# Attention and experts on one core: the chunk's steps in new orders on TensorE, VectorE, ScalarE and GpSimd

## The chip, the cores and the metric

The kernel runs on one core of one Trainium2 chip. The metric is the device time of one execution in microseconds (us). A profiled execution gives the trace; its span runs from the first to the last instruction. "Granted clock" is the share of TensorE's full clock that the chip granted in a stretch; its two levels are 1.2 and 2.4 GHz.

## What is computed

The input `x` is 4 x 2048 tokens of 512 features. The reference, cut to what matters:

```python
# cross attention, 16 heads of 32, 77 context rows of 256
n = layernorm(x)
q, k, v = n @ Wq + bq, ctx @ Wk + bk, ctx @ Wv + bv      # split into heads
a = softmax(q @ k.T / sqrt(32)) @ v                       # 8192 x 16 heads x 77
x = x + concat(a) @ Wo + bo
# experts: every token through one of eight, picked by argmax
n2 = layernorm(x)
e = argmax(n2 @ gate_w.T)
x = x + n2 + expert_w[e] @ n2
```

## The kernel before

The attention runs over 16 chunks of 512 tokens (`NCHUNK`, four per batch), then the tokens, sorted by expert in HBM, go through 72 tiles of 128 rows (from L1430 on). The change touches the attention alone.

Products that need float32 accuracy are made of float16 halves: a matrix is kept as "hi" and "lo", and a product is three matmuls (`product`, L979). ScalarE writes hi from PSUM, VectorE then writes lo, the difference (`lo`, L1218). The kinds of step, with a chunk's group (four heads) and tile (128 tokens) as digits:

- T t: transpose the normalised tokens, split into hi and lo. Q g: query product, split. M g t: scores against the plain keys, of which VectorE takes the negative maximum (L1256). GX: the gate's product with the tokens. These are the front, done for the next chunk.
- NM: transpose the maxima; VectorE copies them to `nmT` (L1260), and SyncE sends them by DMA into the query stack `q_st` (L841). S g j: scores of one head (L1005); ScalarE takes their exponential twice, as float32 `pf` and float16 `p_hi` (L1170, L1171). P g j: `p_lo` = pf - p_hi (L827), j = 0, 1 on VectorE and j = 2, 3 on GpSimd. PV g: probabilities by values, in two halves (L1021); V g h: VectorE divides by the sum (L1241, L1242). These are the core, done for this chunk.
- C t: transpose the attention's result, split. O t: output product, added to x on VectorE (L1277). B t, VE: statistics of the second norm (L1351, L1360, L1362). GC, H, R, SL: gate sums, the argmax and the row of each token in HBM. G, D on GpSimd: row factors (L310 to L312) and the scatter to HBM, four indirect DMAs (L321). These are the tail, done for the chunk before.
- L t, LE, F, X t: statistics, factors and the normalised tokens of the chunk after the next (L1199, L1209, L910 to L913, L1120). A t on GpSimd adds the bias to x (L919). K on VectorE: new keys, once a batch (L334).

One iteration of the software pipeline thus holds the front of chunk i + 1, the core of chunk i and the tail of chunk i - 1. Each engine takes its steps strictly in the order of a table written out by hand: `STEPS` for TensorE (and for SyncE's transfers of q), `VECTOR`, `SCALAR`, `GPSIMD`. The last chunk and the one after it have tables of their own (`_LAST`, `_END`), except on GpSimd. An engine that comes to a step waits on semaphores for its inputs and for its place.

Places set the coupling. Steps of the kinds T, C, NM, Q, M, O, GX, GC and R share four PSUM banks in turn: TensorE can start such a step only when VectorE has done the one four before it (L1031). S steps share two banks (`exp_done`). `pf` is single, so S g j on ScalarE waits for P of the group before (L1163, L1165), and `p_hi` is double, so S g 0 waits for PV of two groups before (L1160). C0 waits for all V steps of its chunk (L1038), NM for all M steps (L1063), S00 for `nmT`'s transfer (L998). SyncE sends a pair of Q groups in 12 transfers (L868) once S13 or S33 is issued. In the first two iterations ScalarE also sums an expert's weights behind each Q step (L1128).

The iterations are a loop of three batches with four chunks each, and the rest written out (`iterations`, L788).

Of the kernel before, what the change touches and what calls it, by code (L numbers as in the profile page):

```python
# [29 lines left out]
H = 16  # L30
# [45 lines left out]
def order(text):  # L76
    names = [(w.rstrip("0123456789"), w) for w in text.split()]
    return [(kind, *(int(d) for d in w[len(kind):])) for kind, w in names]


STEPS = order("""
    NM T0 C0 C1 T1 T2 O0 T3 C2 S00 S01 O1 S02 S03 Q0 S10 S11 C3 O2 S12 M00 M01 S13 Q1 S20 PV0
    S21 M10 GC M11 M12 M13 S22 PV1 S23 M02 S30 Q2 S31 R M03 S32 GX M20 M21 S33 Q3 PV2 M22 M30
    M31 M32 O3 M23 PV3 M33
""")
VECTOR = order("""
    NM T0 C0 C1 T1 T2 K O0 T3 C2 B0 L0 L1 P00 L2 O1 B1 P01 Q0 C3 P10 O2 M00 P11 B2 L3 M01 Q1
    V00 M10 V01 P20 LE GC M11 P21 H M12 M13 M02 V10 Q2 R M03 GX SL M20 P30 V11 M21 Q3 M22 P31
    M30 M31 V20 V21 M32 O3 M23 B3 M33 V30 V31 VE
""")  # L90
SCALAR = order("""
    T0 C0 C1 T1 T2 T3 C2 S00 S01 S02 S03 S10 Q0 C3 S11 S12 S13 Q1 S20 S21 S22 S23 S30 Q2 S31
    X0 S32 X1 Q3 X2 S33 X3
""")
GPSIMD = order("""
    A0 P02 A1 P03 P12 P13 F A2 P22 P23 A3 P32 P33 G D
""")
STEPS_LAST = order("""
    NM C0 C1 C2 C3 O0 S00 S01 O1 S02 S03 O2 S10 S11 GC O3 S12 S13 E00 E01 S20 S21 R PV0 E02 E03 S22 S23 E10 E11
# [1456 lines left out]
```

How the kernel before makes its waits and increments, by code:

```python
    def wait_alone(eng, name, value):  # L203
        eng.wait_ge(sem(name), value)
        eng.sem_inc(sem("waited_alone"))
# [6 lines left out]
        def do(ins):  # L213
            n[0] += 1
            ins.then_inc(sem(name), 1)
            eng.wait_ge(sem(name), n[0])
# [112 lines left out]
    def build_k(b):  # L329
        nc.vector.wait_ge(sem("keys_in"), 16 * (b + 1))
        for j in range(HG):
            src = k_next[0:DK, j:H:HG, :].bitcast(F32)
            ins = nc.vector.tensor_copy(k_cur[j * DK:(j + 1) * DK, :, j * LK:(j + 1) * LK], src)
        ins.then_inc(sem("k_built"), 1)
# [54 lines left out]
        def ready(eng, *u):  # L390
            if u in by_dve:
                eng.wait_ge(sem("prep_dve"), by_dve.index(u) + 1)
            else:
                eng.wait_ge(sem("prep_act"), by_act.index(u) + 1)
# [1 line left out]
        @blk.sync  # L398
# [14 lines left out]
                load(bvec[:, BQ, :], by_feature(bq), "ld_bias")  # L413
            load(wraw["q"][:], Wq.rearrange("(t p) n -> p t n", p=P), "ld_wq")
            load(bo_rep[:], bo.rearrange("(a n) -> a n", a=1).to_broadcast([P, DM]), "ld_bo_rep")
            load(xt[0][:], xv[0], "x_in0")
            sp.wait_ge(sem("prep_dve"), by_dve.index(("k", KT - 1)) + 1)
            for part, half in ((0, 0), (1, 0), (2, 1)):
                for j in range(HG):
# [3 lines left out]
                            .then_inc(sem("k_stacked"), 16)  # L424
            load(xt[1][:], xv[1], "x_in1")
            sp.wait_ge(sem("k_stacked"), 16 * 3 * HG * 2)
            load_keys(sp, 0)
# [55 lines left out]
        @blk.tensor  # L483
        def _(pe):
            pe.wait_ge(sem("ident_ready"), 1)
```

## Time and profile before

| | us |
|---|---|
| three runs | 1070.12, 1072.28 (median), 1076.30 |
| profiled execution | 1070.71 |
| its span | 1068.9 |
| mean granted clock | 0.933 |

| engine | busy us | share of the span |
|---|---|---|
| TensorE (PE) | 948.5 | 89% |
| VectorE (DVE) | 817.8 | 77% |
| GpSimd (POOL) | 554.1 | 52% |
| ScalarE (ACT) | 553.4 | 52% |

TensorE's matmuls are pipelined: a record lasts longer than the engine needs before the next, so its busy time says little about room. On VectorE and ScalarE a record overlaps its successor by some 0.08 to 0.12 us; the price of an instruction in a full queue is the distance from its start to the next start. The attention takes the span up to about 840 us, the expert tiles the rest.

### The profile page before, as it was taken

To read this page: it belongs to the slowest core of one execution; us is meant where nothing else is said; L and a number is where in the kernel's file an instruction comes from. 1 tells how busy PE (TensorE), PEld (TensorE's weight loads), DVE (VectorE), ACT (ScalarE), POOL (GpSimd) and SP (SyncE) were. 2 spreads that over 40 slices of the span, in tenths; PEclk is the share of its full clock that TensorE was granted. 3 is DMA by queue.
4 is the path that set the end of the run, shared out by engine and by line. 5 is a ranking of instruction groups with operands and counts; after the bars stand their busy time and mean duration, and the time that the engine had idled before them with its cause. 6 is when DMAs were issued, how large, how long until landed. Compare 5 with 4: busy or idle time off the path is not lost. (4 is left out here: it accounts for less than half of the span.)

```text
span 1068.9 us, 27389 instructions
## 1 busy us (share of the span) xinstructions
PE 948.5 (89%) x8834; PEld 578.7 (54%) x8835; DVE 817.8 (77%) x1802; ACT 553.4 (52%) x907; POOL 554.1 (52%) x559
## 2 busy tenths in 40 slices
PE   6485799998989999898999999999976699999996
PEld 3342465656656566565665656656564355555553
DVE  7733588899878999897989999888779355566553
ACT  4236775855748567584675855766564121122210
POOL 2412434644555445564455544554555377777774
PEclk9785899999989999998999999999888799999998
DMA  8866626355453544545446255443933456565551
GB/s 240 243 161 174 146 79 157 79 141 120 129 142 91 139 109 125 142 106 142 98 131 166 68 157 119 122 121 82 276 130 120 120 172 169 162 176 170 164 173 35
DMA packets 85687, 149.53 MB, mean 140 GB/s; under 512 B 22849, under 2 KB 24693, under 8 KB 85567
## 3 DMA queue, kind: packets, MB, share of 16 engines
q1 hardware_dynamic: 73359, 111.89, 42.3%
q0 software_dynamic: 11664, 36.05, 8.8%
q8 instruction: 72, 1.18, 0.5%
q14 instruction: 48, 0.39, 0.1%
q10 hardware_dynamic: 544, 0.02, 0.0%
HBM read 58.65 MB, written 40.50 MB: 93 GB/s over the span
## 5 line engine op out<-in xcount | busy, mean ns | idle before, releaser
L827 POOL TENSOR_TENSOR p_lo<-pf,p_hi 77x512 f16<-77x512 f32 x128 | 160.3, 1260 | 194.6 <-ACT p_hi L1171 193.3
L1170 ACT ACTIVATE pf<-scoresT,exp_scale 77x512 f32<-77x512 f32 x256 | 174.9, 683 | 43.9 <-PE scoresT L1005 30.1
L1477 PE MATMUL mo<-e_w,x2T_hi 128*128 x576 | 184.2, 381 | 0.8 <-DVE x2T_lo L1514 0.8
L1171 ACT ACTIVATE p_hi<-scoresT,exp_scale 77x512 f16<-77x512 f32 x256 | 174.8, 683 | 0.0
L1497 ACT ACTIVATE x2T_hi<-mt 128x512 f16<-128x512 f32 x72 | 43.1, 598 | 183.7 <-PE mt L1466 183.7
L827 DVE TENSOR_TENSOR p_lo<-pf,p_hi 77x512 f16<-77x512 f32 x128 | 120.0, 938 | 7.1 <-ACT p_hi L1171 7.1
L1005 PE MATMUL scoresT<-q_st,k_now 97*77 97x512 f32 x256 | 112.4, 472 | 14.5 <-ACT p_hi L1171 11.0
L1524 DVE SCALAR_TENSOR_TENSOR res<-mo,inv,row 128x512 f32<-128x512 f32 x72 | 54.1, 751 | 91.3 <-PE mo L1477 91.3
L1256 DVE TENSOR_REDUCE negmax<-work 128x4 f32<-128x308 f32 x256 | 115.2, 468 | 4.4 <-PE work L1053 2.7
L1151 ACT ACTIVATE xnT_hi<-work 128x512 f16<-128x512 f32 x64 | 37.3, 596 | 146.0 <-PE work L991 145.5
L1477 PE MATMUL mo<-e_w,x2T_lo 128*128 x288 | 109.9, 382 | 0.0
L982 PE MATMUL work<-xnT_hi,wq_hi 128*128 128x512 f16 x256 | 101.3, 396 | 5.5 <-DVE xnT_lo L1234 5.5
L1448 POOL DMA_INDIRECT out<-res,row x72 | 71.5, 994 | 64.9 <-DVE xn L1509 56.7
L1021 PE MATMUL pv<-v_now_hi,p_hi 96*128 96x33 f16 x1024 | 86.7, 179 | 19.4 <-DVE cc L1242 15.9
L982 PE MATMUL work<-wo_hi,cT_hi 128*128 128x512 f16 x256 | 99.0, 387 | 1.9
L982 PE MATMUL work<-xnT_hi,wq_lo 128*128 128x512 f16 x256 | 100.2, 391 | 0.0
L982 PE MATMUL work<-xnT_lo,wq_hi 128*128 128x512 f16 x256 | 99.9, 390 | 0.0
L982 PE MATMUL work<-wo_hi,cT_lo 128*128 128x512 f16 x256 | 97.9, 382 | 0.0
L982 PE MATMUL work<-wo_lo,cT_hi 128*128 128x512 f16 x256 | 97.5, 381 | 0.0
L1021 PEld LDWEIGHTS pv<-v_now_hi,p_hi 96*128 96x128 f16 x1024 | 79.5, 96 | 33.3 <-DVE cc L1242 16.7
L1440 POOL TENSOR_TENSOR row<-row,xn 128x512 f32<-128x512 f32 x72 | 86.3, 1200 | 15.2 <-DVE xn L1509 13.7
L1229 DVE SCALAR_TENSOR_TENSOR q_lo<-work,bq_s,q_hi 128x512 fp32r<-128x512 f32 x64 | 47.9, 749 | 57.8 <-ACT q_hi L1147 57.8
(228 smaller groups left out, 2330.4 us busy)
## 6 DMA issues: line engine op xcount, KB each, us to landing
q_st<-q_hi SPq DMA_DIRECT2D x256, 128.0 KB, 2.4
row<-rows_by_expert SPq DMA_DIRECT2D x72, 257.5 KB, 3.0
xt<-in_x SPq DMA_DIRECT2D x16, 1024.0 KB, 6.3
q_st<-q_lo SPq DMA_DIRECT2D x128, 128.0 KB, 2.5
pay<-in_L_ffn_expert_w SPq DMA_DIRECT2D x8, 1024.0 KB, 7.2
er<-in_L_ffn_expert_w SPq DMA_DIRECT2D x7, 1024.0 KB, 15.4
k_next<-key_stacks SPq DMA_DIRECT2D x5, 462.0 KB, 9.8
key_stacks<-k_nat_hi SPq DMA_DIRECT2D x8, 154.0 KB, 3.3
```

What stands on the lines that cost most here:

```text
L827: return tt.tensor_tensor(pp[1][0:LK, g % 2, j, :], pf[:, j, :], pp[0][0:LK, g % 2, j, :], ALU.subtract)
L982: ins = nc.tensor.matmul(dst, a[ia], bm[ib], start=first and n == 0, stop=final and n == 2)
L1005: nc.tensor.matmul(sbank[n % SB][0:LK, :], k_now[0:KR, n, :], q_st[0:KR, n, :], start=True, stop=True)\
L1021: ins = nc.tensor.matmul(obank[h][:, col:col + VC], pp[ip][:, g % 2, j, t * P:(t + 1) * P], v_now[iv][:, g * HG + j, :], start=n == 0, sto ...
L1170: nc.scalar.activation(pf[:, j, :], sbank[n % SB][0:LK, :], ACT.Exp, scale=exp_scale[0:LK, :])
L1171: nc.scalar.activation(pp[0][0:LK, g % 2, j, :], sbank[n % SB][0:LK, :], ACT.Exp, scale=exp_scale[0:LK, :]).then_inc(sem("exp_done"), 1)
L1229: ins = nc.vector.scalar_tensor_tensor(out=q[1][:, at, :], in0=ps[:, :], scalar=bq_s[:, at:at + 1], in1=q[0][:, at, :].bitcast(F32), op0=A ...
L1256: return nc.vector.tensor_reduce(negmax[:, t, g * HG:(g + 1) * HG], ps[:, 0:HG * LK].rearrange("p (j s) -> p j s", j=HG), X, ALU.max, nega ...
L1440: nc.gpsimd.tensor_tensor(row[:, u, 0:DM], row[:, u, 0:DM], xn2[:, u, :], ALU.add)\
L1448: nc.gpsimd.indirect_dma_start(out=out_rows, out_offset=bass.IndirectOffsetOnAxis(ap=row[:, u, C_ID:C_ID + 1].bitcast(I32), axis=0), in_=r ...
L1477: ins = nc.tensor.matmul(obank2[u % 2][:, :], x2T[ia][:, u % 2, k, :], w, start=k == 0 and n == 0, stop=k == KT - 1 and n == 2)
L1524: nc.vector.scalar_tensor_tensor(out=res[:, u, :], in0=obank2[u % 2][:, :], scalar=inv[:, S_E:S_E + 1], in1=row[:, u, 0:DM], op0=ALU.mult, ...
```

## The change

Only the four tables of the full iteration change. The same steps stand in them, each on the engine it was on. `_LAST` and `_END` tables and all functions stay.

```diff
 STEPS = order("""
-    NM T0 C0 C1 T1 T2 O0 T3 C2 S00 S01 O1 S02 S03 Q0 S10 S11 C3 O2 S12 M00 M01 S13 Q1 S20 PV0
-    S21 M10 GC M11 M12 M13 S22 PV1 S23 M02 S30 Q2 S31 R M03 S32 GX M20 M21 S33 Q3 PV2 M22 M30
-    M31 M32 O3 M23 PV3 M33
+    T0 T1 NM C0 T2 C1 T3 O0 C2 S00 S01 Q0 S02 S03 O1 S10 M00 C3 S11 M01 Q1 S12 PV0 S13 M02 GC M03 M10 S20 S21 M11 M12
+    O2 M13 S22 S23 Q2 R S30 S31 PV1 M20 Q3 S32 M21 S33 M22 PV2 M23 O3 M30 GX PV3 M31 M32 M33
 """)
 VECTOR = order("""
-    NM T0 C0 C1 T1 T2 K O0 T3 C2 B0 L0 L1 P00 L2 O1 B1 P01 Q0 C3 P10 O2 M00 P11 B2 L3 M01 Q1
-    V00 M10 V01 P20 LE GC M11 P21 H M12 M13 M02 V10 Q2 R M03 GX SL M20 P30 V11 M21 Q3 M22 P31
-    M30 M31 V20 V21 M32 O3 M23 B3 M33 V30 V31 VE
+    T0 T1 NM C0 T2 C1 K T3 O0 B0 P00 P01 C2 Q0 O1 M00 B1 L0 C3 M01 L1 P10 P11 L2 Q1 M02 GC M03 L3 M10 M11 H P20 LE P21
+    M12 V00 V01 O2 M13 B2 Q2 R V10 V11 M20 SL P30 Q3 V20 M21 M22 M23 V21 P31 O3 M30 B3 GX VE V30 M31 M32 M33 V31
 """)
 SCALAR = order("""
-    T0 C0 C1 T1 T2 T3 C2 S00 S01 S02 S03 S10 Q0 C3 S11 S12 S13 Q1 S20 S21 S22 S23 S30 Q2 S31
-    X0 S32 X1 Q3 X2 S33 X3
+    T0 T1 C0 T2 C1 T3 S00 S01 C2 Q0 S02 S03 C3 S10 S11 Q1 S12 S13 S20 S21 S22 S23 Q2 X0 S30 S31 Q3 S32 X1 X2 S33 X3
 """)
 GPSIMD = order("""
-    A0 P02 A1 P03 P12 P13 F A2 P22 P23 A3 P32 P33 G D
+    A0 A1 A2 P02 P03 A3 P12 P13 F P22 P23 P32 P33 G D
 """)
```

## Rows read from the trace of the kernel before

**Rows 1.** The chain that ended last, by engine.
```profile
PE 21%; DVE 0%; issue 0%; POOL 0%; ACT 0%; POOLq 0%; DVEq 0%
```
**Rows 2.** Stretches: us, busy us (x instructions) by engine, clock, DMA share, GB/s.
```profile
134.20:751.30 617.10, 577.52 (x6528) 367.14 (x6527) 548.33 (x1277) 400.84 (x668) 314.97 (x313) 0.96 0.48 120
...
358.40:401.20 42.80, 40.29 (x465) 25.27 (x464) 38.67 (x92) 28.38 (x48) 22.84 (x23) 0.98 0.49 125
```
**Rows 3.** Timeline, VectorE: start, us, instruction, [idle before, releaser]; first and last wait.
```profile
363.21 0.75 DVE L1277 SCALAR_TENSOR_TENSOR pay<-work,inv_y,xt 128x512 f32<-128x512 f32 x1 [1.14 <-PE work L982]
...
386.12 0.75 DVE L1229 SCALAR_TENSOR_TENSOR q_lo<-work,bq_s,q_hi 128x512 fp32r<-128x512 f32 x1 [0.98 <-ACT q_hi L1147]
```
**Rows 4.** Timeline, VectorE: a long p_lo, a long and a short gate step.
```profile
369.98 1.79 DVE L827 TENSOR_TENSOR p_lo<-pf,p_hi 77x512 f16<-77x512 f32 x1
...
387.88 1.33 DVE L1266 SCALAR_TENSOR_TENSOR gx<-gx,inv,gate_c 128x32 f32<-128x32 f32 x1
...
739.75 0.25 DVE L1266 SCALAR_TENSOR_TENSOR gx<-gx,inv,gate_c 128x32 f32<-128x32 f32 x1
```
**Rows 5.** Timeline, GpSimd, at the same times.
```profile
369.95 1.27 POOL L919 TENSOR_TENSOR xt<-xt,bo_rep 128x512 f32<-128x512 f32 x1
...
387.89 1.26 POOL L919 TENSOR_TENSOR xt<-xt,bo_rep 128x512 f32<-128x512 f32 x1
```
**Rows 6.** The page's groups: count, busy us, mean ns, idle before and releaser.
```profile
L827 DVE TENSOR_TENSOR p_lo<-pf,p_hi 77x512 f16<-77x512 f32 x128 | 120.0, 938 | 7.1 <-ACT p_hi L1171 7.1
```
**Rows 7.** Timeline, VectorE, a full queue: Q, C, P, O, M; then NM.
```profile
372.32 0.75 DVE L1229 SCALAR_TENSOR_TENSOR q_lo<-work,bq_s,q_hi 128x512 fp32r<-128x512 f32 x1 [0.55 <-ACT q_hi L1147]
372.99 0.68 DVE L1234 TENSOR_TENSOR cT_lo<-work,cT_hi 128x512 f16<-128x512 f32 x1
373.59 0.68 DVE L827 TENSOR_TENSOR p_lo<-pf,p_hi 77x512 f16<-77x512 f32 x1
374.19 0.74 DVE L1277 SCALAR_TENSOR_TENSOR pay<-work,inv_y,xt 128x512 f32<-128x512 f32 x1
374.85 0.46 DVE L1256 TENSOR_REDUCE negmax<-work 128x4 f32<-128x308 f32 x1
...
401.19 0.68 DVE L1260 CAST nmT<-work 16x512 fp32r<-16x512 f32 x1
```
**Rows 8.** Timeline, TensorE: O0, T3, C2, Q0, second half of PV2, NM.
```profile
360.42 0.38 PE L982 MATMUL work<-wo_hi,cT_hi 128*128 128x512 f16 x1
...
363.00 0.60 PE L991 MATMUL work<-ident,xn 128*128 128x128 f32 x4
363.44 0.27 PE L991 MATMUL work<-ident,cc 128*128 128x128 f32 x1
...
367.43 0.39 PE L982 MATMUL work<-xnT_hi,wq_hi 128*128 128x512 f16 x1
...
392.35 0.19 PE L1021 MATMUL pv<-v_now_hi,p_hi 96*128 96x33 f16 x1 [0.92 <-DVE cc L1242]
...
399.67 0.92 PE L1065 MATMUL work<-ident,negmax 128*16 128x128 f32 x4 [1.36 <-DVE negmax L1256]
```
**Rows 9.** Timeline, SyncE's queue.
```profile
401.89 0.56 SPq L841 DMA_DIRECT2D q_st<-nmT  x1
```
**Rows 10.** The transfers of tile nmT, all 16 of them.
```profile
DMA to landing us min/median/max: 2.7/2.7/5.6
```
**Rows 11.** Timeline, GpSimd: the first scatter of the chunk.
```profile
404.21 1.08 POOL L321 DMA_INDIRECT rows_by_expert<-pay,slot  x1 [0.94 <-POOL pay L312]
```
**Rows 12.** Timeline, ScalarE: the expert sum behind the last Q before chunk 0.
```profile
79.50 1.91 ACT L1128 ACTIVATE pay<-pay 128x2048 f32<-128x2048 f32 x1 [6.23 <-DMA pay<-in_L_ffn_expert_w]
```
**Rows 13.** Stretches, as rows 2: two ends of a chunk.
```profile
353.50:360.40 6.90, 5.34 (x76) 4.04 (x75) 6.76 (x21) 2.19 (x4) 1.39 (x3) 1.00 0.82 179
396.30:404.00 7.70, 6.34 (x77) 5.74 (x76) 7.00 (x21) 2.01 (x4) 1.48 (x3) 0.78 0.76 165
```
**Rows 14.** The scatter's line L321, its 64 transfers.
```profile
DMA to landing us min/median/max: 3.0/4.8/9.1
```

## The prediction

> **What bounds the kernel now.** I read the chain of waits first, and it misleads: it names only TensorE's expert phase after 840 us [rows 1], which this change leaves alone. So I cut the span by chunk. From the first NM step with a tail to the last chunk's, fourteen chunks take 617.1 us; a clean one takes 42.8 [rows 2]; the mean is 44.1, because two chunks carry a loop's return, three carry new keys and the clock falls at some chunk ends, none of which the change touches. Only this stretch can move, and it is 14 of 16 chunks.
>
> In the clean chunk TensorE's records cover 40.3 us and VectorE's 38.7, so neither is simply the bound. The timeline of VectorE settles it. It waits five times, 1.14 us first and 0.98 last, 3.3 in all [rows 3]. It also loses time inside its own instructions. The p_lo subtraction at 369.98 takes 1.79 us where the same one at 373.59 takes 0.68, and the gate step at 387.88 takes 1.33 where it takes 0.25 at 739.75 [rows 4, 7]. Each time GpSimd is in the middle of an addition, from 369.95 and from 387.89 [rows 5]. Both instructions read two SBUF tensors; VectorE's other long ones read PSUM or one tensor and keep their length. The group of VectorE's p_lo has a mean of 938 ns [rows 6], so eight a chunk lose 8 x (0.94 - 0.68) = 2.1 us and the gate step 1.33 - 0.25 = 1.1: 3.2 us of the chunk. What remains is VectorE's real work, 42.8 - 3.3 - 3.2 = 36.3 us.
>
> From the last Q to the end of the chunk VectorE has no wait, and TensorE waits for it: 0.92 us inside PV2 (behind the gate step) and 1.36 before NM [rows 8]. Earlier in the chunk TensorE is full and VectorE waits. So the chunk is two halves with different bounds, and VectorE's losses fall in the half where it is the bound.
>
> **The change part by part.** No instruction is added, so the cost is in four queues walked side by side. I put zero at the start of the product O0 on TensorE.
>
> 1. Front half. Today O0 starts at 360.42 and the eighth step behind it at 367.43, 7.0 us for one heavy product, T3, C2, another product and four S [rows 8]. In the new order T3 stands before O0 (a T step is 0.44, from 363.00 to 363.44); so O1 starts at 6.6. A product of twelve matmuls takes 2.4 and drains 0.4: VectorE can take O1 at 9.4. Between C0, whose end lets O0 start, and O1 it has T2, C1, T3, O0, B0, P00, P01, C2 and Q0: with the start-to-start prices of 0.60 for T, C, P and B, 0.66 for O and 0.67 for Q [rows 7] that is 5.5 us of work in 9.5. VectorE is idle 4.0 us here, and this is the only place.
>
> 2. GpSimd. A0 to A2 now run in one block before P02. Its scatter ends near 3.1 (worked out below), the three additions of 1.27 us [rows 5] fill 3.1 to 6.9, and P00 and P01, due at 4.8 and 6.0, each wait for the addition under way: 0.6 and about 1.3 us. They end at 7.9, C2 and Q0 at 9.2, before O1. So this collision is hidden, with 0.2 to spare; without that cover it would cost up to 1.9. A3 meets only L, M and C steps. P10, P11 come when GpSimd waits for S12; P20, P21 between P13 and F; P30 after P23; P31 between P32 and P33; and no A is left beside the gate step. I value what still collides at 0, the nearest row being the clean 0.68 of a p_lo with GpSimd idle, and bound it by 0 and 3.2 (all of today's loss).
>
> 3. Back half. From O1 to the C0 of the next chunk VectorE has 36.3 - 5.5 = 30.8 us without a wait of its own if TensorE stays ahead. TensorE reaches Q2's end at 23.3 and VectorE Q2 at 24.0; Q3 28.2 against 28.6; O3 32.9 against 32.6; PV3 starts at 34.0, V30 at 35.6. They run neck and neck, and the small waits (Q3, V20, O3) are regained behind PV3. C0 ends at 9.4 + 30.8 = 40.2, and O0 starts 0.1 later. That is the new clean chunk: 40.3 for 42.8, or equally 36.3 of work plus 4.0 idle. Gain 2.5.
>
> 4. The chunk's end. T0 and T1 now fill TensorE's 1.36 us before NM. TensorE then waits for VectorE step by step (0.1 to 0.4 at T1, NM, C0, C1, T3), about 1.4 in all; this is in the 40.3.
>
> 5. ACT. Q0's copy stands before S02, S30 waits for PV1 (about 2 us idle at 24). S00 to S03 are ready before S10 and S11 need their banks, and by my walk S33 ends at 32.5. P33 on GpSimd ends at 33.7, 0.3 before PV3. Zero, but thin: each further microsecond there is a microsecond of the chunk.
>
> 6. nmT's transfer. NM moves behind T0 and T1, its copy starts 1.3 before O0, SyncE issues 0.7 later (401.19 to 401.89) and it lands 2.7 later [rows 7, 9, 10]: at 2.1, with S00 at 3.0. The slack falls from 1.3 to 0.9. Two queues move past each other here: VE now precedes V30, so the row factors and the scatter start some 4 us earlier. Today the first scatter is issued at 404.21, 2.3 us after nmT's transfer [rows 11]; now four of them, 1.27 apart, start from about -1.9 and bracket it. SyncE's twelve q transfers end near 37.5, well before. I take no stall; the bounds are 0 and the stall of the third rival.
>
> 7. Ends. The last chunk's own table starts with NM, so the last edge keeps its 1.36: I count 1.1 gained there. In chunk 0, NM now waits for T1, and T1 for an xn step that the new order of ScalarE puts behind the expert sum at 79.50, which itself waited 6.23 us for its transfer [rows 12]. The cost is between 0 and 6.2; I take 2, as nmT's transfer is late there already.
>
> The sum: 13 x 2.5 + 1.1 - 2 = 31.6 us less. A walk laid by hand assumes no late hand-over; I give back 0.2 a chunk, 2.8 us, since two engines run level over 30 us. 1070.7 - 28.8 = 1042. The profiled execution took 1070.71 us, 1.6 under the median of the three runs and within their spread, so the same number serves for a run.
>
> **The clock, weighed.** The end of a chunk took 6.9 us with a granted clock of 1.00 (353.5 to 360.4) and 7.7 at 0.78 (396.3 to 404) [rows 13]: at such an end the transposes and small matmuls, and TensorE's wait, let it fall to the lower of 1.2 and 2.4 GHz. In the new order O3 ends and O0 starts 7.7 us apart, with GX, PV3, three M and seven transposing steps between, but with less idle time in one piece. I take today's share of lowered ends.
>
> The Trainium skill, "TensorE: Matmul & The Clock Gate", Part 4, says that a transpose does not count as a busy engine in the same way, which speaks against seven such steps in a row. This case's rows show only that six steps of that kind and a wait of 1.36 lowered it at one end and not at another. If the rule decides, the second rival below holds; if the idle time decides, the forecast.
>
> **The rivals.** *The collisions move instead of going.* The gate step is freed, P00 and P01 are covered, but the six other p_lo keep today's mean loss of 0.26: 1.6 us a chunk in the half where VectorE is the bound, 14 x 1.6 = 22: 1064. For it: P10, P30 and P31 have under a microsecond between them and a GpSimd start in my walk. Against: GpSimd's p_lo follow S steps that come later. Chance 0.12.
>
> *The lower clock at every end.* The rows price 22 hundredths over 7.7 us at 0.8 us; half clock through a whole end is 1.8, some 1.3 more than today's average: 14 x 1.3 = 18: 1060. Chance 0.08.
>
> *Slower: the scatter in front of nmT.* Place: nmT's transfer among four scatters, whose own landing is 3.0 to 9.1 us, median 4.8 [rows 14]. S00 stalls TensorE by the landing less 3.6. At 4.8 that is 1.2 a chunk, 1059; at 5.7 the gain is gone, and beyond it the change loses; at 7.0, midway to the longest, 3.4 x 14 = 48: 1090. For it: nothing was between them before. Against: it goes by another queue, and it landed in 2.7 beside the row load of xt. Chance 0.06.
>
> *Nothing gained.* ScalarE's chain (5) or a bank not free in time takes the place of the losses: 1070, chance 0.06. The forecast has 0.68.
>
> **How the numbers follow.** Low end: no allowance and hardly a lowered clock, 1032. High end: the first rival with a little over, 1066. Half a per cent, 5.4 us, is about what a measurement of this kernel can tell from no change. Faster by more than that: the forecast, most of the first two rivals, 0.85. Within: 0.08. Slower: 0.07.
>
> **What would show it.** A clean chunk of 40 to 41 us; the gate step at 0.25 and the mean p_lo on VectorE near 0.9, with P00 and P01 the long ones; no 1.36 us wait before NM and no 0.92 inside PV2; VectorE's one long idle piece between B0 and O1. Wrong: nmT landing above 3.6 with TensorE waiting at S00; VectorE idle behind O1; PV3 waiting for GpSimd; the clock at an end under 0.7 throughout.

## The result, and the profile after

The changed kernel takes 1034.08 us (median of four runs, 1033.00 to 1038.95), the kernel before 1071.20 beside it (four runs, 1066.78 to 1076.30): a ratio of 0.966, 95% interval 0.961 to 0.971. The forecast was 1042 with a range of 1032 to 1066. All readings below are from the profiled execution: 1033.0 us, span 1031.1, mean granted clock 0.947 (before 0.933). In the kernel after, every line number is 3 lower: the p_lo subtraction is L824, the gate step L1263, the copy to `nmT` L1257.

Stretches, as in [rows 2]: the same fourteen chunks, then a clean one, then the two pieces at 1.2 GHz that are left in the fourteen.

```profile
135.10:713.90 578.80, 562.90 (x6514) 354.60 (x6513) 511.78 (x1276) 401.83 (x666) 305.68 (x314) 0.99 0.52 128
343.64:384.19 40.55, 40.08 (x469) 25.09 (x467) 36.72 (x92) 29.02 (x49) 22.20 (x24) 1.00 0.56 136
297.30:304.10 6.80, 5.56 (x25) 4.88 (x26) 2.79 (x5) 2.39 (x4) 5.86 (x6) 0.50 0.64 205
464.60:471.40 6.80, 5.33 (x25) 4.95 (x26) 2.80 (x5) 2.39 (x4) 5.38 (x6) 0.50 0.64 204
```

The fourteen chunks fall from 617.1 to 578.8, 38.3 less. They start 0.9 later (135.1 for 134.2), and what follows the last `nmT` copy is 0.4 shorter: 37.8 in all, the difference of the spans. So the gain lies in the fourteen. A clean chunk falls from 42.78 to 40.55, by 2.23, and VectorE's records in it from 38.67 to 36.72 with the same 92 instructions: it loses 1.95 less inside instructions. That the two numbers are alike proves nothing, since experiment 4 takes another 1.45 out of VectorE's records and gains nothing.

The page's group of VectorE's p_lo, as [rows 6]:

```profile
L824 DVE TENSOR_TENSOR p_lo<-pf,p_hi 77x512 f16<-77x512 f32 x128 | 104.8, 834 | 18.3 <-ACT p_hi L1168 16.9
```

The mean fell from 938 to 834 ns, not to 680. Where the rest is, VectorE's timeline of the clean chunk shows (start, us, instruction, idle before and releaser):

```profile
343.64 0.67 DVE L1257 CAST nmT<-work 16x512 fp32r<-16x512 f32 x1
...
347.84 0.75 DVE L1274 SCALAR_TENSOR_TENSOR pay<-work,inv_y,xt 128x512 f32<-128x512 f32 x1 [1.14 <-PE work L979]
...
349.91 2.95 DVE L824 TENSOR_TENSOR p_lo<-pf,p_hi 77x512 f16<-77x512 f32 x2 [0.59 <-ACT p_hi L1168]
...
353.39 0.73 DVE L1226 SCALAR_TENSOR_TENSOR q_lo<-work,bq_s,q_hi 128x512 fp32r<-128x512 f32 x1
354.42 0.75 DVE L1274 SCALAR_TENSOR_TENSOR pay<-work,inv_y,xt 128x512 f32<-128x512 f32 x1 [0.30 <-PE work L979]
...
364.39 0.69 DVE L824 TENSOR_TENSOR p_lo<-pf,p_hi 77x512 f16<-77x512 f32 x1
...
372.36 0.17 DVE L1366 CAST slot<-slotf 128x4 int32<-128x4 f32 x1
...
373.88 0.75 DVE L1226 SCALAR_TENSOR_TENSOR q_lo<-work,bq_s,q_hi 128x512 fp32r<-128x512 f32 x1 [0.34 <-ACT q_hi L1144]
...
378.06 0.75 DVE L1274 SCALAR_TENSOR_TENSOR pay<-work,inv_y,xt 128x512 f32<-128x512 f32 x1 [0.53 <-PE work L979]
...
379.92 0.25 DVE L1263 SCALAR_TENSOR_TENSOR gx<-gx,inv,gate_c 128x32 f32<-128x32 f32 x1
```

And GpSimd's, at the same time:

```profile
347.97 3.74 POOL L916 TENSOR_TENSOR xt<-xt,bo_rep 128x512 f32<-128x512 f32 x3
353.36 2.31 POOL L824 TENSOR_TENSOR p_lo<-pf,p_hi 77x512 f16<-77x512 f32 x2 [1.65 <-ACT p_hi L1168]
```

P00 and P01 together take 2.95 where two clean ones take 1.28. They end at 352.86, just over a microsecond after the third addition (347.97 + 3.74 = 351.71). P00 alone pays: it starts 1.94 us into the run of three, in the second addition, and gets nowhere until the third is over. But C2 and Q0 behind it are done at 354.12, and O1, the next result that TensorE delivers, is not there until 354.42. Over the fourteen chunks p_lo still loses 17.7 us, in eleven P00 and one P31; the gate step lost 12.7 before and now loses nothing in any chunk.

A third instruction lost time before, and the prediction doesn't name it: the cast of the row numbers in step SL (L1369, now L1366), a short one with one SBUF input. In the clean chunk before, it and P31 stand beside p_lo steps of GpSimd (VectorE, then GpSimd):

```profile
389.56 0.88 DVE L1369 CAST slot<-slotf 128x4 int32<-128x4 f32 x1
...
393.79 1.50 DVE L827 TENSOR_TENSOR p_lo<-pf,p_hi 77x512 f16<-77x512 f32 x1
```
```profile
389.26 1.15 POOL L827 TENSOR_TENSOR p_lo<-pf,p_hi 77x512 f16<-77x512 f32 x1
...
393.58 1.15 POOL L827 TENSOR_TENSOR p_lo<-pf,p_hi 77x512 f16<-77x512 f32 x1 [3.17 <-ACT p_hi L1171]
```

The cast takes 0.17 in the changed kernel; before, it lost 0.7 us in each of the fourteen chunks, about 10 us in all.

TensorE's timeline of the chunk's end, as [rows 8], and the stretch with its clock, as [rows 13]:

```profile
381.87 0.65 PE L988 MATMUL work<-ident,xn 128*128 128x128 f32 x4 [0.41 <-DVE negmax L1253]
382.56 0.60 PE L1062 MATMUL work<-ident,negmax 128*16 128x128 f32 x4
383.13 0.66 PE L988 MATMUL work<-ident,cc 128*128 128x128 f32 x4
...
385.60 0.38 PE L979 MATMUL work<-wo_hi,cT_hi 128*128 128x512 f16 x1
```

```profile
376.50:384.20 7.70, 7.23 (x127) 5.48 (x125) 7.03 (x22) 3.31 (x6) 3.13 (x5) 1.00 0.85 191
```

The waits of 1.36 before NM and 0.92 inside PV2 have become one of 0.41 and several short ones that the list doesn't show: the six steps from 381.87 to O0 at 385.60 start 0.62 apart on average, where a T step takes 0.44 without a wait, so they hold about 1.1 us more. The granted clock stays at 1.00 through an end that had 0.78. Time at half clock inside the fourteen chunks fell from 43.7 to 13.8 us. What is left is nearly all in the two pieces above, both at a loop's return.

The transfers of `nmT`, as [rows 10]:

```profile
DMA to landing us min/median/max: 2.7/2.7/4.0
```

### The profile page after: what moved, and what is told of

Same layout as the page of the kernel before. It is cut to its first block and busy times, and to the rows that moved or that the text cites. A ratio compares the mean times of both kernels' runs of the same rounds, so it can differ in the third digit from the quotient of the medians.

```text
span 1031.1 us, 27389 instructions
## 1 busy us (share of the span) xinstructions
PE 934.9 (91%) x8834; PEld 567.6 (55%) x8835; DVE 783.3 (76%) x1802; ACT 555.8 (54%) x907; POOL 546.4 (53%) x559
## 5 line engine op out<-in xcount | busy, mean ns | idle before, releaser
L824 POOL TENSOR_TENSOR p_lo<-pf,p_hi 77x512 f16<-77x512 f32 x128 | 148.6, 1166 | 239.8 <-ACT p_hi L1168 239.7
L1002 PE MATMUL scoresT<-q_st,k_now 97*77 97x512 f32 x256 | 105.9, 463 | 14.4 <-ACT p_hi L1168 11.2
L824 DVE TENSOR_TENSOR p_lo<-pf,p_hi 77x512 f16<-77x512 f32 x128 | 104.8, 834 | 18.3 <-ACT p_hi L1168 16.9
L1253 DVE TENSOR_REDUCE negmax<-work 128x4 f32<-128x308 f32 x256 | 112.7, 469 | 6.5 <-PE work L1050 6.4
L1474 PEld LDWEIGHTS mo<-e_w,x2T_hi 128*128 128x128 f16 x576 | 56.7, 98 | 61.7 <-issue 2.8
L1018 PE MATMUL pv<-v_now_lo,p_hi 96*128 96x33 f16 x1024 | 84.3, 178 | 0.0
```

The lines of the kernel that those rows point to most:

```text
L824: return tt.tensor_tensor(pp[1][0:LK, g % 2, j, :], pf[:, j, :], pp[0][0:LK, g % 2, j, :], ALU.subtract)
L1002: nc.tensor.matmul(sbank[n % SB][0:LK, :], k_now[0:KR, n, :], q_st[0:KR, n, :], start=True, stop=True)\
L1018: ins = nc.tensor.matmul(obank[h][:, col:col + VC], pp[ip][:, g % 2, j, t * P:(t + 1) * P], v_now[iv][:, g * HG + j, :], start=n == 0, sto ...
L1253: return nc.vector.tensor_reduce(negmax[:, t, g * HG:(g + 1) * HG], ps[:, 0:HG * LK].rearrange("p (j s) -> p j s", j=HG), X, ALU.max, nega ...
L1474: ins = nc.tensor.matmul(obank2[u % 2][:, :], x2T[ia][:, u % 2, k, :], w, start=k == 0 and n == 0, stop=k == KT - 1 and n == 2)
```

## The experiments

All ran with the kernel before beside them on one chip (1072.7 to 1073.5 us). Of each, the two quantities that tell most are the clean chunk (one with no loop's return and no new keys) and the three chunks with new keys, 3, 7 and 11, called key chunks. These take 40.97, 40.95 and 40.97 in the changed kernel and 44.34, 45.10 and 45.04 in the one before.

**1. GpSimd's new table alone, in the kernel before.**

```diff
-    A0 P02 A1 P03 P12 P13 F A2 P22 P23 A3 P32 P33 G D
+    A0 A1 A2 P02 P03 A3 P12 P13 F P22 P23 P32 P33 G D
```

> The kernel before, with the new GpSimd table alone (A0 to A2 ahead of P02, A3 ahead of P12); the other three tables as they were. Theory A (the collisions of VectorE with GpSimd cost time where VectorE is the bound, behind the last Q, and nothing where TensorE is): the gate step L1266 falls from 1.33 to 0.25 us in every chunk, TensorE's 0.92 us wait inside PV2 goes, and a clean chunk falls from 42.8 to 41.7 us, with the rest (the wait before NM, P30 and P31) unchanged: 1071 - 14 x 1.1 = 1056 us. Theory B (the gain comes from T0 and T1 ahead of NM, which fill TensorE's 1.36 us): the GpSimd table is worth nothing, 1071 us.

It took 1114.41 us, ratio 1.040 (1.036 to 1.044): slower. The gate step is indeed 0.25 in all chunks. But VectorE's P00 has a new length. VectorE, then GpSimd, then ScalarE, of one chunk:

```profile
374.27 6.71 DVE L827 TENSOR_TENSOR p_lo<-pf,p_hi 77x512 f16<-77x512 f32 x1
```
```profile
373.24 3.75 POOL L919 TENSOR_TENSOR xt<-xt,bo_rep 128x512 f32<-128x512 f32 x3
376.92 2.28 POOL L827 TENSOR_TENSOR p_lo<-pf,p_hi 77x512 f16<-77x512 f32 x2
379.16 1.27 POOL L919 TENSOR_TENSOR xt<-xt,bo_rep 128x512 f32<-128x512 f32 x1
```
```profile
381.10 0.68 ACT L1170 ACTIVATE pf<-scoresT,exp_scale 77x512 f32<-77x512 f32 x1 [4.29 <-DVE p_lo L827]
```

P00 starts a microsecond into GpSimd's run and ends at 380.98, half a microsecond after the last of six GpSimd instructions (380.43): it got in between none of them. ScalarE needs the place of `pf` and waits 4.29 us for it. p_lo's loss in the fourteen chunks is 81.1 us, against 31.2 before. So the GpSimd table alone is no gain; it needs the VectorE order that brings P00 late.

**2. The changed kernel with GpSimd's old table.** The diff of experiment 1, reversed.

> The changed kernel with the old GpSimd table: only the four A steps stand among the p_lo as before. Theory A: an addition falls again beside the late steps of VectorE (A2 and A3 behind F and P23, near SL, P30 and Q3); each collision in the stretch from O1 to the next C0 is paid in full, so a clean chunk rises from 40.55 by 0.5 to 1.1 us and the time from 1034 to 1041 to 1050 us; the sum over VectorE's p_lo and gate records beyond 0.68 and 0.25 us, behind O1, equals the rise. Theory B: 1034 us.

1043.81 us, ratio 0.973 (0.970 to 0.976). The time is about what the collisions' theory gave, but the theory looked at the wrong instructions: p_lo loses only 1.9 us in all fourteen chunks and the gate step 0.2. The collisions came in step SL, whose cast takes 0.96 for 0.17 in twelve of the fourteen chunks and whose product with the one-hot rows mostly takes 0.6 for 0.18, here in the chunk from 178.55:

```profile
207.55 0.61 DVE L1364 TENSOR_TENSOR lg<-lg,oh 128x32 f32<-128x32 f32 x1
...
208.41 0.97 DVE L1366 CAST slot<-slotf 128x4 int32<-128x4 f32 x1
```

That is 1.2 us lost. In chunk 7 the loss is the same and nothing waits for `nmT`: VectorE's waits before Q3 and O3 (0.35 and 0.53 in the changed kernel) are gone, which takes up 0.9 of it, and the chunk is longer by the rest, 41.28 for 40.95. The other part is the transfers of `nmT` and TensorE's wait for them:

```profile
DMA to landing us min/median/max: 2.7/3.5/4.7
```
```profile
183.67 0.66 PE L1002 MATMUL scoresT<-q_st,k_now 97*77 97x512 f32 x2 [0.52 <-DMA q_st<-nmT]
```

Of this chunk's 1.03 us over the changed kernel's, 0.52 is S00 waiting for `nmT`, the stall of the slower rival at a small size. In all TensorE waits there 5.5 us, five times, against 3.2, twice; of these, four and one lie in the fourteen chunks, 0.5 to 1.1 us each and 0.41. Why `nmT` lands later was not settled. The order on GpSimd doesn't show as the reason: the first scatter is issued 1.2 us ahead of `nmT` here as in the changed kernel, and in experiment 6, with the changed kernel's own GpSimd table, `nmT` also lands up to 4.4 us after its issue. How the 8.4 us over the changed kernel's fourteen chunks divide between the two causes was not measured apart.

**3. NM back in front, nothing else.**

```diff
 STEPS and VECTOR
-    T0 T1 NM C0 T2 C1
+    NM T0 T1 C0 T2 C1
```

> The changed kernel with NM again ahead of T0 and T1 on TensorE and VectorE. Theory A: TensorE waits some 1.4 us before NM again, but VectorE is the bound there and loses only what it waits for NM's transposes behind V31, 0.3 to 0.6 us a chunk: 1034 + 14 x 0.4 = 1040 us. Theory B: a full 1.36 us a chunk, 1053 us. The granted clock at the chunk ends, now at its upper level at all but two, tells whether the undivided wait or the transposes lower it: by the wait it falls again at most ends, by the transposes it stays as it is.

1060.48 us, ratio 0.988 (0.985 to 0.991): 26 of the 37 us are gone, more than either theory allowed. Three prices show. TensorE has its undivided wait again, and at six of the twelve ordinary ends the clock falls, as it does at both loop's returns: the clean chunk with it, and the one without it.

```profile
394.83 0.60 PE L1062 MATMUL work<-ident,negmax 128*16 128x128 f32 x4 [1.55 <-DVE negmax L1253]
```
```profile
353.43:395.47 42.04, 40.41 (x468) 26.25 (x467) 35.53 (x91) 28.79 (x48) 22.30 (x23) 0.97 0.52 128
528.85:570.11 41.26, 39.59 (x468) 25.15 (x467) 36.20 (x90) 28.79 (x48) 22.32 (x23) 1.00 0.52 129
```

So NM's place is worth 41.26 - 40.55 = 0.7 us at full clock and 0.8 more where the clock falls; half clock inside the chunks is 47.0 us again. The third price is in the key chunks (45.75, 46.98, 46.99). VectorE and GpSimd there:

```profile
399.85 5.08 DVE L331 CAST k_cur<-k_next 32x308 fp32r<-32x308 f32 x3
```
```profile
401.01 3.73 POOL L916 TENSOR_TENSOR xt<-xt,bo_rep 128x512 f32<-128x512 f32 x3
```

K, the cast of new keys from SBUF to SBUF, now meets the run of additions; one of its pieces takes 4.42 us instead of 0.31, and TensorE's Q0 waits up to 3.5 for T3's lo behind it. In the changed kernel K ends just before A0 starts.

**4. The additions moved off P00, in the changed kernel.**

```diff
-    A0 A1 A2 P02 P03 A3 P12 P13 F P22 P23 P32 P33 G D
+    A0 P02 P03 A1 A2 P12 P13 A3 F P22 P23 P32 P33 G D
```

> The changed kernel with another GpSimd table: A0 P02 P03 A1 A2 P12 P13 A3 F P22 P23 P32 P33 G D. The long P00 (2.3 us, waiting for A0 to A2) goes. Theory A: P00 lies in VectorE's idle stretch before O1, so nothing is gained: a clean chunk stays at 40.55 and the time at 1034 (A1, A2 end at 13.0 by the walk, just before P10 at 13.3; if they meet, up to +1). Theory C (every lost VectorE microsecond counts, wherever it is): 1.7 us a chunk less, 1010 us.

1034.96 us, ratio 0.965 (0.961 to 0.968), as the change itself. p_lo's loss falls from 17.7 to 1.8 us and the clean chunk stays at 40.56:

```profile
344.14:384.70 40.56, 40.08 (x469) 25.07 (x467) 35.27 (x91) 29.02 (x49) 22.19 (x24) 1.00 0.55 134
```

VectorE's records are 1.45 us shorter for nothing. What P00 still loses in the changed kernel is free.

**5, 6 and 7. One more instruction on VectorE, at three places.** Each repeats a statistic that is computed anyway (0.60 us from start to start) and changes no result that is used.

```diff
 VECTOR, one in each
+    B0 Y P00        # 5: in the front
+    B2 Y Q2         # 6: in the middle
+    M30 Y B3        # 7: behind O3
```

> The changed kernel with one more instruction on VectorE in each chunk with a tail: a fifth bn_stats of 0.60 us (of pay's tile 0, into a place that B3 overwrites later), between B0 and P00. Theory A (VectorE has idle time between T3 and O1, TensorE is the bound there): it falls into the 0.59 us wait before P00, a clean chunk stays at 40.55, the time at 1034. Rival (VectorE is the bound all along): 0.60 us a chunk, 14 x 0.6 = 8.4 us, 1043.

> The same bn_stats (of tile 2) between B2 and Q2, behind O1. Theory A (VectorE is the bound from O1 to the next C0): paid in full or nearly, 0.5 to 0.6 us a chunk, a clean chunk of 41.1, 1034 + 14 x 0.55 = 1042 us; more than that if it sends the clock down at the chunk ends. Rival (TensorE is the bound of the changed kernel throughout): nothing, 1034.

> The changed kernel with one more bn_stats of 0.60 us on VectorE (of pay's tile 2, into a free place of bst) between M30 and B3, behind the product O3. The run with the same instruction between B2 and Q2 cost nothing in a clean chunk (40.56), so VectorE is not the bound from O1 on as theory A had it. Theory D: TensorE is the bound from O0 to the end of O3, and VectorE only from O3 to the next C0; its waits before Q3 (0.34) and O3 (0.53) took up the 0.60. Then the same instruction behind O3, where VectorE has no wait left, costs its full 0.60 us a chunk: a clean chunk of 41.15, 1034 + 8.4 = 1042 us, and more where the longer end sends the clock down. Rival (VectorE has hidden room there too, TensorE or a transfer is the bound throughout): 40.55, 1034.

The clean chunks of the three:

```profile
135.83:176.38 40.55, 40.07 (x469) 25.04 (x467) 35.63 (x92) 29.03 (x49) 15.07 (x17) 1.00 0.44 105
```
```profile
178.31:218.86 40.55, 40.07 (x468) 25.05 (x467) 37.40 (x92) 29.02 (x49) 22.18 (x24) 1.00 0.55 134
```
```profile
346.95:388.10 41.15, 40.19 (x469) 25.04 (x467) 37.29 (x92) 29.03 (x49) 22.21 (x24) 1.00 0.54 130
```

Number 5: 1033.58 us, ratio 0.964 (0.960 to 0.968), free as the forecast's walk says. Number 6: 1036.41, ratio 0.966 (0.961 to 0.970), and free too, which the forecast's walk excluded: it made VectorE the bound from O1 on. (Its four runs lie between 1033.0 and 1039.1; in the profiled one, 1039.05, the chunk from 346.31 takes 41.59 with a wait of 0.84 for `nmT`.) The timeline of number 6 shows where its 0.6 us went: Q3 has no wait and O3 a shorter one.

```profile
208.72 0.74 DVE L1226 SCALAR_TENSOR_TENSOR q_lo<-work,bq_s,q_hi 128x512 fp32r<-128x512 f32 x1
...
212.73 0.75 DVE L1274 SCALAR_TENSOR_TENSOR pay<-work,inv_y,xt 128x512 f32<-128x512 f32 x1 [0.37 <-PE work L979]
```

Number 7, behind O3: 1041.62, ratio 0.973 (0.969 to 0.976), a clean chunk of 41.15, exactly 0.60 longer. So VectorE has room in front of O3 and none from O3 to the next C0. That TensorE is what bounds the chunk before O3 is read from its timeline, where the only wait over 0.15 us in the clean chunk is the 0.41 at its end; no instruction was added to TensorE to test it.

**8. The kernel before, with its additions at the end of GpSimd's chunk.**

```diff
-    A0 P02 A1 P03 P12 P13 F A2 P22 P23 A3 P32 P33 G D
+    P02 P03 P12 P13 F P22 P23 P32 P33 A0 A1 A2 A3 G D
```

> The kernel before, with GpSimd's four additions moved behind P33, where VectorE has no step with two SBUF inputs: P02 P03 P12 P13 F P22 P23 P32 P33 A0 A1 A2 A3 G D. The collisions of the additions go; P01 and P31 can still meet GpSimd's own p_lo. Theory A (collisions behind the last Q cost in full): the gate step is 0.25 in every chunk, the wait inside PV2 goes, a clean chunk falls by 1.1 to 1.5 us to 41.3 to 41.7, the batch chunks too, 1071 - 14 x 1.3 = 1053 us. If the collisions were not what the change removed: 1071.

1051.15 us, ratio 0.981 (0.977 to 0.985): some 21 of the 37 us, with the old order on the three other engines. Its clean chunk:

```profile
350.57:391.78 41.21, 40.28 (x470) 25.16 (x469) 35.17 (x92) 28.94 (x49) 23.26 (x23) 1.00 0.51 130
```

p_lo's loss is 4.5 us, the gate step's none, and half clock in the chunks is 23.3 us. The cast in SL is at 0.17 and P31 at 0.68, so 1.57 us of a clean chunk went with the collisions. TensorE's two waits account for it: the 0.92 inside PV2 is gone, and the 1.36 before NM is 0.70. The rest, 41.21 - 40.55 = 0.66 a chunk, is the new order. That wait stands in its old place, ahead of all transposes, and the clock stays at 1.00 at the ends of the clean chunks:

```profile
390.08 0.60 PE L1065 MATMUL work<-ident,negmax 128*16 128x128 f32 x4 [0.70 <-DVE negmax L1256]
```

The key chunks are 43.22: there the copy of the values, 0.28 us otherwise, meets the additions (GpSimd's run is the four from 429.25 to 434.20).

```profile
432.29 2.07 DVE L345 COPY v_now_hi<-v_all_hi 96x528 f16 x1
434.28 0.28 DVE L345 COPY v_now_lo<-v_all_lo 96x528 f16 x1
```

**9. Two more statistics in VectorE's idle stretch.** On VectorE L0 goes behind P01 and L1 behind Q0; for that the row load of xt, 1 MB, is issued ahead of `nmT` on SyncE. GpSimd's table is that of experiment 4.

```diff
-    B0 P00 P01 C2 Q0 O1 M00 B1 L0 C3 M01 L1 P10 P11
+    B0 P00 P01 L0 C2 Q0 L1 O1 M00 B1 C3 M01 P10 P11
```

> A version meant to beat the changed kernel: L0 moved behind P01 and L1 behind Q0 on VectorE (into its idle stretch before O1), SyncE sends the load of xt before nmT instead of behind it, so that the rows are there, and GpSimd's table is A0 P02 P03 A1 A2 P12 P13 A3 F P22 P23 P32 P33 G D, so that P00 meets nothing. Theory A: 1.2 us of VectorE's work leave the stretch in which it is the bound; TensorE, 0.5 to 1 us behind it, then takes over: a clean chunk of 39.6 to 40.0, 1034 - 14 x 0.7 = 1024 us. Rival (the load of 1 MB ahead of nmT delays its landing beyond the 0.9 us of slack, as the scatter did in the run with the old GpSimd table): TensorE waits before S00 and the time is 1034 or more, with nmT's landing above 3.6 us.

1097.84 us, ratio 1.021 (1.015 to 1.028): slower than the kernel before. The transfers of `nmT`, and what line L1002 (S) waited for:

```profile
DMA to landing us min/median/max: 2.7/7.5/8.7
```
```profile
  DMA q_st<-nmT: 55.2, 15
```

Most of its chunks take 46 to 48 us (a clean one 46.68; the first of the fourteen, where nothing waits for `nmT`, 40.55). Twelve of the fourteen wait for `nmT`, 0.9 to 5.1 us each and 45 in all, and time at half clock rises to 63 us. This is the stall of the slower rival at full size, with the megabyte load, issued about 1 us ahead, in front of `nmT` besides the scatter: the 32 KB land 7.5 us after issue (median) instead of 2.7.

**10. NM second instead of third, T3 last.**

```diff
-    T0 T1 NM C0 T2 C1 T3 O0
+    T0 NM C0 T1 T2 C1 T3 O0
```

> A version meant to beat the changed kernel: the chunk begins T0 NM C0 T1 T2 C1 T3 O0 (TensorE), with VectorE and ScalarE in the same order, instead of T0 T1 NM C0 T2 C1 T3 O0. Theory D: the end of the chunk is VectorE's chain from O3 to C0, and T1 (0.60 us) leaves it; NM has only T0 ahead of it, so TensorE waits some 0.4 us more before NM, undivided for about 0.9. Net 0.3 to 0.5 us a chunk less, 40.1 to 40.2, and nmT is sent 0.6 earlier; 1034 - 5 = 1029 us. Rival (one transposing step does not fill TensorE's wait for M33, VectorE then waits for NM's transposes, and the clock falls at more ends, as with NM first): 0.3 to 1.5 us a chunk more, 1040 to 1050 us.

1034.38 us, ratio 0.966 (0.963 to 0.970), no change. TensorE waits longer before NM, but the clock falls only at the loop's returns, as in the changed kernel:

```profile
382.78 0.60 PE L1062 MATMUL work<-ident,negmax 128*16 128x128 f32 x4 [1.11 <-DVE negmax L1253]
```
```profile
343.04:383.81 40.77, 39.48 (x468) 25.11 (x467) 36.58 (x91) 28.77 (x48) 22.30 (x23) 1.00 0.53 128
```

A clean chunk is 0.2 longer. T1, T2, C1 and T3 now stand between C0 and O0, which is the likely reason. No version beats the change.

## Why the prediction was right, and where its reasons were not

**What bounded the kernel before: right in kind, with the losses in the wrong places.** The collisions of VectorE with GpSimd are real: taking them away alone gives some 21 us (experiment 8) and 1.57 us of a clean chunk, not 3.2. I had spread a mean over eight p_lo. In fact six of them are clean, and P01 (1.79) and P31 (1.50) are long. P01 stands ahead of three of VectorE's waits (0.55, 0.33, 0.98), so by the timeline its 1.1 us fell where VectorE had time (no run took it away alone); the rival with "today's mean loss of 0.26" on six p_lo priced a loss that those six never had. Behind Q2, where VectorE has no wait, the losses were the gate step's 1.1, P31's 0.8, and 0.7 of the cast in SL, which I had missed: I looked at the long instructions only.

The Trainium skill, "SBUF — State Buffer", section "Who interferes with whom", says that a VectorE instruction with two SBUF inputs, or a copy or cast in a mode that uses both ports, contends with GpSimd for a port pair. The rows here agree: p_lo, the gate step and the product in SL (two inputs), K, the cast in SL and the values' copy are the ones that grow, and statistics of one tensor keep 0.68 beside the additions. The same section says, of the modes that use both ports, that whoever issues first keeps the pair for the whole instruction. Here the loser was often shut out for longer than that: P00 through the rest of one addition and all of the next (2.35 us for 0.68), in experiment 1 through six GpSimd instructions (6.71).

**Part 1, the front half: right to 0.1 us.** O0 to O1 on TensorE was 6.57 (345.05 to 351.62) for 6.6; VectorE took O1 at 9.4 for 9.4.

**Part 2, the additions beside P00 and P01: the wrong reason with the right verdict.** I shared the loss between the two, 0.6 and 1.3, "each for the addition under way". In fact P00 waits for the whole run, 1.67 us over its clean length, and P01 runs clean. The sum was close (1.7 for 1.9), and the cover held. Experiment 1 shows what was at stake: waiting for the addition under way alone would have cost P00 some 0.3 us there, and it lost 6.0.

**Part 3, the back half: the step that failed.** The forecast put VectorE's one idle piece in front of O1, "and this is the only place", and VectorE as the bound from there to C0. Experiment 6 costs nothing where that says 0.6 a chunk, and experiment 7 costs 0.60. VectorE has room until O3 and is the bound only from O3 to C0. The sum came out because two errors cancel. The forecast had 30.8 us of VectorE's work and no wait from O1 to the end of C0. Measured are 31.0 (354.42 to 385.46), of which 0.87 is waiting, so 30.2 of work. The 0.6 that is missing has the size of the collision in SL, which the 36.3 us of "real work" still contained. That the work was too long by about as much as the waits were left out is luck. The two engines ran level, as forecast: on VectorE Q2 came at 24.3 behind O0 (forecast 24.0), Q3 at 28.8 (28.6), O3 at 33.0 (32.6) and V30 at 35.6 (35.6). I had named the small waits at Q3 and O3 and taken them as regained; they are what hides more work there. The clean chunk is 40.55 for the forecast's 40.3 and its 0.2 of allowance.

**Parts 4 and 7, the ends: under-sized.** Of the 38.3 us the forecast had 30.8 (13 x 2.5 + 1.1 - 2.8). Clean chunks gave 2.23 each, for 2.3. The other 7.5 came from chunks that it had taken as equal to them. The three key chunks gave 3.4, 4.1 and 4.1. In the kernel before, P31 there meets GpSimd's cast of the key stack, which I had not looked for and which costs it 1.15 us more than in a clean chunk:

```profile
437.32 2.65 DVE L827 TENSOR_TENSOR p_lo<-pf,p_hi 77x512 f16<-77x512 f32 x1
```
```profile
437.12 1.15 POOL L827 TENSOR_TENSOR p_lo<-pf,p_hi 77x512 f16<-77x512 f32 x1 [3.17 <-ACT p_hi L1171]
438.22 1.21 POOL L340 CAST k_now<-k_next 96x1232 fp32r<-96x1232 f32 x1
```

Against 2.3 each that is 4.7 more. These chunks also had 3.2 to 4.1 us at half clock before and have none now, and the two causes were not measured apart. The first of the fourteen chunks gave 4.6, or 2.3 more, with a fall of the clock in it before and none after; the others together 0.5 more. TensorE's waits at the chunk's end are 0.41 and about 1.1 in short pieces, for "about 1.4 in all". Chunk 0 was as told in kind: its T1 waits 4.9 us for xn behind the expert sum and its NM is 7.3 later, but the chunk is 6.4 shorter, so 0.9 is left of the 2 that I took.

**The clock: the forecast took today's share, and it fell.** Half clock in the chunks went from 43.7 to 13.8 us. What that is worth is open. In experiment 3 a chunk with 2.1 us at half clock is 0.8 longer than one with none (42.04 against 41.26); at that rate the 29.9 us less are some 11 us, an estimate. But in the kernel before, the clean chunk without any (179.38 to 222.16) takes 42.78 and the two with 1.4 and 1.7 us at half clock take 42.79 and 42.78, and at that rate they are nothing. The rival of the clock at every end is refuted: there are seven steps of small transposes in a row, and the clock is 1.00. The Trainium skill, "TensorE: Matmul & The Clock Gate", Part 4, says that a transpose does not count as a busy engine in the same way. If that decided here, experiment 3, which has the same seven steps in another order, would do no worse than the change. What differs is the wait ahead of them. At some 1.55 us, undivided, the clock falls at six of the twelve ends that are no loop's return. At 0.41, or 1.11 behind one transposing step, it falls at none of them. At 0.70 in the same place as the 1.55 (experiment 8) it falls only behind two key chunks, where a further wait of 2.3 us follows. That speaks for the length of the wait and not its place. The length alone doesn't settle it either, since the same 1.55 left the clock up at the other six.

**Part 6, `nmT`'s transfer: right, and thinner than it looks.** Cast 1.4 before O0, issue 0.7 later and landing 2.7 later are the forecast's numbers. The slower rival came in one of the fourteen chunks of this kernel, with 0.41 us, where `nmT` landed 4.0 after its issue. Experiments 2 and 9 bring its stall in at 0.5 to 1.1 us in four chunks and at up to 5.1 in twelve. The rival of the moved collisions did not come: P10 to P30 are clean in every chunk, P31 is long in one, and the place of P00 is free (experiment 4).

In short: about 21 us come from collisions that are gone, and the rest goes with the new order on the three other engines, with a wait cut in pieces, a clock that stays up, and no new collision of K or the values. Only the first part was tried alone; the split of the rest is by chunk sizes, not by a run of its own.

## What to carry to other kernels

Lost time inside an instruction, seen as one record longer than its like, is to be priced as a wait is: by where it falls. P00's loss of 1.67 us cost nothing where VectorE was ahead (experiment 4); its loss of 6.0 us where ScalarE waited for the result cost 3.9 us of a chunk (experiment 1, 46.71 for 42.79, part of it at half clock). A group's mean hides which instructions lose: look at each record, the short ones too. Test which engine bounds a stretch by adding one small instruction to it, at more than one place: a level walk does not tell. And look at the odd chunks (a batch's first, a loop's return) on their own before taking them as equal to a clean one.

## What the runs showed of the hardware that was not expected

- A VectorE instruction that collides with GpSimd can be shut out through several GpSimd instructions that follow each other without a wait: 2.35 us through the rest of one addition and the next, 6.71 through six instructions, a cast of 4.42 for 0.31, a copy of 2.07 for 0.28. It isn't always so. The P01 of [rows 4], due since 369.98, was over 0.55 us after the addition of [rows 5], though GpSimd's next instruction started at once, and that one (shown below) took 1.60 for 1.15. It went so in all fourteen chunks of the kernel before. What decides whether VectorE gets in between two instructions, no run here shows.

```profile
371.19 1.60 POOL L827 TENSOR_TENSOR p_lo<-pf,p_hi 77x512 f16<-77x512 f32 x1
```

- A transfer of 32 KB that SyncE issues about 1 us behind one of 1 MB lands 7.5 us after its issue instead of 2.7 (medians, experiment 9).
- Seven transposing steps in a row left TensorE at 2.4 GHz; with one wait of 1.55 us ahead of them it fell to 1.2 at half of the ordinary ends (experiment 3), with one of 0.70 at no end of a clean chunk (experiment 8).
